# A macaron block on one core: pair 0 projected a stage earlier, ten of its maxima units in the last stages, the second phase's x split inside the last batch, and opposite bank orders for even and odd batches

## The reference, cut to what matters

```python
x = x + 0.5 * ffn(layernorm(x))        # x: 16 x 256 x 128
x = x + attn(layernorm(x))             # 16 heads of 8
x = x + 0.5 * ffn(layernorm(x))        # the same weights

def ffn(x):                            # ternary weights, one scale per output
    h = silu(tlin(x, w1)) * tlin(x, w2)        # 128 -> 512
    h = gelu(tlin(h, h1)); h = gelu(tlin(h, h2))   # 512 -> 512, exact gelu
    return tlin(h, w3)                         # 512 -> 128
def attn(x):
    q, k, v = proj(x, Wq, bq), proj(x, Wk, bk), proj(x, Wv, bv)
    return softmax(q k^T / sqrt(8)) v @ Wo.T + bo  # per head
```

## Time and profile before

| | us |
|---|---|
| median of the timed runs (3) | 666.66 (664.96 to 670.3) |
| the profiled execution's own time | 672.58 |
| its span | 670.8 |
| PE, DVE, ACT, POOL busy | 630.9, 440.4, 466.8, 92.4 |
| mean granted clock of PE | 0.949 |

### The profile page before, as it was taken

The page is one execution under the profiler, slowest core; times in us unless marked ns, Lnnn a source line. Parts: engine busy times, 40 slices in busy tenths (PEclk is TensorE's granted clock), DMA queues, the critical chain, the costliest instruction groups (busy, mean ns, idle before and its releaser), DMA issues.

```text
span 670.8 us, 12974 instructions
## 1 busy us (share of the span) xinstructions
PE 630.9 (94%) x4452; PEld 462.1 (69%) x4452; DVE 440.4 (66%) x1036; ACT 466.8 (70%) x791; POOL 92.4 (14%) x256
## 2 busy tenths in 40 slices
PE   1969999999999799999999999999999999999996
PEld 1748878788776566666666566666567878878785
DVE  4844666858545867877878887784076485656742
ACT  2646786968864357777777868774477796887964
POOL 2601010012101012222222222102001001010000
PEclk9969999999999679999999999995689999999999
DMA  9100000000051704370715343300000001001011
GB/s 296 41 2 1 1 0 0 1 0 0 1 195 56 251 2 153 101 245 13 249 62 189 118 133 127 128 1 1 1 3 1 1 0 33 0 0 31 1 31 33
DMA packets 36674, 41.97 MB, mean 63 GB/s; under 512 B 2448, under 2 KB 27280, under 8 KB 36624
## 3 DMA queue, kind: packets, MB, share of 16 engines
q1 hardware_dynamic: 36624, 41.31, 18.2%
HBM read 22.42 MB, written 18.87 MB: 62 GB/s over the span
## 4 chain that ended last, share of the span: by engine, by line
PE 82%; DVE 7%; ACT 4%; issue 3%; DMA 2%; POOL 0%; SPq 0%; ACTq 0%; POOLq 0%
PE bank L1008 45%; PE bank L1118 10%; PE bank L1092 7%; PE bank L1105 5%; PE bank L1107 4%; DVE neg_max L816 2%; PE bank L1150 2%; PE bank L1136 2%; ACT probs L630 1%; PE bank L1081 1%; PE bank L1073 1%; PE bank L1055 1%; DVE act_lo L766 1%; PE bank L1077 1%; DMA QK<-qk_scratch 1%
## 5 line engine op out<-in xcount | busy, mean ns | idle before, releaser
L1008 PE MATMUL bank<-act_hi,WH 128*128 128x512 f32 x576 | 233.3, 405 | 6.8 <-issue 5.4
L1008 PE MATMUL bank<-act_lo,WH 128*128 128x512 f32 x576 | 228.8, 397 | 0.0
L816 DVE TENSOR_REDUCE neg_max<-bank 128x2 f32<-128x512 f32 x256 | 166.9, 682 | 50.0 <-PE bank L1092 46.8
L630 ACT ACTIVATE probs<-bank 128x512 f32<-128x512 f32 x256 | 140.8, 597 | 54.6 <-PE bank L1107 52.5
L786 DVE TENSOR_TENSOR act_lo<-full,act_hi 128x512 fp32r<-128x512 f32 x128 | 88.0, 689 | 124.2 <-ACT act_hi L529 124.1
L527 ACT ACTIVATE full<-bank,SG 128x512 f32<-128x512 f32 x128 | 88.0, 687 | 69.1 <-PE bank L1008 68.7
L1008 PEld LDWEIGHTS bank<-act_hi,WH 128*128 128x128 f32 x576 | 109.1, 189 | 37.2 <-issue 6.0
L1008 PEld LDWEIGHTS bank<-act_lo,WH 128*128 128x128 f32 x576 | 109.1, 189 | 25.4 <-issue 0.5
L1105 PE MATMUL bank<-QK 32*128 32x256 f32 x512 | 113.0, 348 | 3.5 <-ACT probs L630 1.8
L1107 PE MATMUL bank<-m_parts,SEL 32*128 32x256 f32 x512 | 96.0, 293 | 0.0
L1092 PE MATMUL bank<-QK 32*128 32x256 f32 x512 | 83.1, 340 | 6.7 <-DVE neg_max L816 4.8
(11 more groups left out here) (91 smaller groups left out, 597.2 us busy)
## 6 DMA issues: line engine op xcount, KB each, us to landing
qk_scratch<-qk SPq DMA_DIRECT2D x64, 256.0 KB, 2.6
QK<-qk_scratch SPq DMA_DIRECT2D x16, 1024.0 KB, 7.2
X<-x SPq DMA_DIRECT2D x4, 512.0 KB, 6.9
raw_rest<-w_ffn SPq DMA_DIRECT2D x4, 512.0 KB, 6.1
out<-X SPq DMA_DIRECT2D x4, 512.0 KB, 3.2
raw<-w_ffn SPq DMA_DIRECT2D x3, 256.0 KB, 4.4
WA<-w_att SPq DMA_DIRECT2D x1, 256.0 KB, 5.2
xT<-sel SPq DMA_DIRECT2D x1, 256.0 KB, 5.1
```

The lines of the kernel that those rows point to most:

```text
L630: A.activation(probs[:, v % 8, :], bank[B_BANKS[v]][:, :], ACT.Exp, scale=SCALE)\
L816: D.tensor_reduce(neg_max[:, bb, qt, n0:n0 + 2], bank[banks[u]][:, :].rearrange("p (h k) -> p h k", h=2), axis=AX.X, op=ALU.max, negate=Tr ...
L1008: ins = MM(dst, a, b, start=k == 0, stop=k == len(todo) - 1)
```

## The change

- The last body of phase 0: transposes and bias product of pair 0 behind tile 0 of stage one, q behind tile 1, k behind tile 2, V behind tile 2 of stage two; the last product's high part goes ahead of the xT copy on ACT, the outputs of the body before move to its places 2 and 3. Maxima units 0 to 3 of batch 0 in stage three, 4 to 9 in stage four, 10 to 15 between the outputs.
- Pair 1's q and k go to `qk_full` and its low parts to POOL, ahead of `max_again(0, 0)`; the transposes of y come after all units.
- Bank orders: 16 units at distance three, odd batches in the opposite order; `used_last` searches through the batch before.
- V projection of the next pair (and its evacuation) from u = 7 to u = 9.
- Statistics for the second phase at u = 2 to 6 of batch 15, `normalise` at u = 10; the transposes at u = 15 of batch 15 into banks 1 and 5, ACT's split at u = 1, 2 of `attend(16)`, DVE's ahead of the addition of batch 14. POOL doubles batch 15's maxima ahead of the rsqrt. ACT's evacuation of batch 15's o is in layer 1 behind tile 0.

```diff
-A_BANKS = (0, 1, 5) * 4 + (0, 1, 5, 1)
-B_BANKS = (2, 3, 7) * 4 + (2, 3, 7, 3)
+A_BANKS = ((0, 1, 5) * 5 + (0,), (5, 1, 0) * 5 + (5,))
+B_BANKS = ((2, 3, 7) * 5 + (2,), (7, 3, 2) * 5 + (7,))
...
+        def used_last(banks, prev, u):
+            before = prev + banks[:u]
+            return next((d for d in range(1, len(before) + 1) if before[-d] == banks[u]), u + 1)
...
             pool.wait_ge(att_in, 16 * N_ATT_CONSTS)
+            low_parts(1)
             max_again(0, 0)
...
+            max_again(NBATCH - 1, 1)
             rsqrt_steps(NORMS1, K * NORMS1)
-            max_again(NBATCH - 1, 1)
...
+                        side = {0: first_x_to_sbuf, 1: lambda: high_q(0, 1), 2: first_k,
+                                3: lambda: output(before + 1, 1)}
                     hidden(g, 0, 0, side)
-                    hidden(g + HT, 0, 1, {1: lambda: high_q(0, 1), 2: lambda: high_k(0, 2)} if into_att else {})
-                    hidden(g + 2 * HT, 1, 0, {0: lambda: set_v(0, 0, 3)} if into_att else {})
+                    hidden(g + HT, 0, 1, {3: lambda: set_v(0, 0, 3)} if into_att else {})
+                    hidden(g + 2 * HT, 1, 0)
...
-                            high_q(1, 5)
-                            high_k(1, 4)
+                            full_part(1, 0, 5)
+                            high_part(1, 0)
+                            full_part(1, 1, 4)
+                            high_part(1, 1)
...
-                    layer1(t1, {3: lambda: o_to_sbuf(NBATCH - 1)})
+                    layer1(t1, {0: lambda: evacuate_o(NBATCH - 1), 3: lambda: o_to_sbuf(NBATCH - 1)})
...
-                    if u == 7 and v_pair is not None:
+                    if u == 9 and v_pair is not None:
                         set_v(*v_pair)
...
-                    if u == steps - 1 and not own:
+                    if u in (1, 2) and not own:
                         act.wait_ge(qk_written, WRITES * NPAIR)
-                        split_x(NB, 0)
-                        split_x(NB + 1, 1, 5)
+                        split_x(NB + u - 1, u - 1, (1, 5)[u - 1])
...
-                attend(2 * i + 1, 1, prev2=not first, more=more, norm=norm)
+                if more:
+                    attend(2 * i + 1, 1, prev2=not first, norm=norm)
+                else:
+                    attend(2 * i + 1, 1, more=False, steps=norm_steps(NORMS1, 0, biased=4), steps_at=2,
+                           norm=(NORMS1, 0, 8), norm_at=10)
...
+            low_x(NB, 0, 1)
+            low_x(NB + 1, 1, 5)
             add_att(NBATCH - 2, 2 * NBATCH - 4)
-            low_x(NB, 0)
-            low_x(NB + 1, 1, 5)
...
-                    hidden(g, 0, 0, h_lo, hl + HT, general, {2: tokens} if into_att else {})
+                    hidden(g, 0, 0, h_lo, hl + HT, general,
+                           {0: tokens, 1: lambda: project_q(0, 1), 2: lambda: project_k(0, 2)} if into_att else {})
...
+                    hidden(g + HT, 0, 1, h_lo, hl + 2 * HT, general, back | ({2: entry_v} if into_att else {}))
+                    hidden(g + 2 * HT, 1, 0, g_lo, g + HT + SLOTS, general,
+                           {1: lambda: entry(0), 2: lambda: entry(1, 2), 3: lambda: entry(3)} if into_att else {})
...
-                           {0: lambda: entry(0, 1), 1: lambda: entry(2), 2: lambda: entry(3, 4),
-                            3: lambda: entry(5)} if into_att else {})
+                           {0: lambda: entry(4, 5), 1: lambda: entry(6), 2: lambda: entry(7, 8),
+                            3: lambda: entry(9)} if into_att else {})
...
+                    if u == 0 and own and not prev:
+                        pe.wait_ge(q_full, 1)
+                        pe.wait_ge(k_full, 1)
...
                     if u == 1 and own and not prev:
+                        pe.wait_ge(x_added, NB + CREDIT)
                         rows_of_max()
...
-                    if u == steps - 1 and not own:
-                        pe.wait_ge(att_added, b - 1)
-                        transpose_x(XN1, 0)
+                    if u == UNITS - 1 and not more and own:
+                        transpose_x(XN1, 0, 1)
                         transpose_x(XN1 + 1, 1, 5)
-                    if u == 7 and v_pair is not None:
+                    if u == 9 and v_pair is not None:
```

More of the change, by code:

```diff
@@ L644, in o_to_sbuf, with attend @@
                 A.activation(onT[:, :], bank[6][:, 0:SEQ], ACT.Copy).then_inc(on_T_sb, 1)
-            def attend(b, prev=True, prev2=True, own=True, steps=UNITS, ahead=None, v_pair=None):
+            def attend(b, bb, prev=True, prev2=True, own=True, steps=UNITS, ahead=None, v_pair=None):
                 for u in range(steps):
@@ L651, in attend @@
                         if v < UNITS:
-                            exp_unit(b - d, v)
-                        if v == UNITS + 3:
+                            exp_unit(b - d, (bb + d) % 2, v)
+                        if v == UNITS + 3 and own:
                             evacuate_o(b - d)
@@ L682, in _ @@
             att_body(NPAIR - 1, 1, ahead=False, more=False)
-            attend(NBATCH, own=False, steps=SKEW + 4)
+            attend(NBATCH, 0, own=False, steps=SKEW + 4)
             ffn_phase(1)
@@ L816, in max_unit @@
                 D.tensor_reduce(neg_max[:, bb, qt, n0:n0 + 2],
-                                bank[banks[u]][:, :].rearrange("p (h k) -> p h k", h=2), axis=AX.X,
+                                bank[(banks or A_BANKS[bb])[u]][:, :].rearrange("p (h k) -> p h k", h=2), axis=AX.X,
                                 op=ALU.max, negate=True).then_inc(max_done, 1)
@@ L944, in _, with attend @@
             ffn_phase(0)
-            def attend(b, bb, prev=True, prev2=True, more=True, steps=(), norm=None):
+            def attend(b, bb, prev=True, prev2=True, more=True, steps=(), steps_at=7, norm=None, norm_at=3):
                 for u in range(UNITS):
@@ L956, in attend @@
                         add_att(b - 2, 2 * b - 4)
-                    if u == 3 and norm is not None:
+                    if u == norm_at and norm is not None:
                         n, tile0, width = norm
@@ L961, in attend @@
                             normalise(n, tile0 + 4, 4)
-                    if u >= 7:
-                        for step in steps[u - 7:u - 6]:
+                    if u >= steps_at:
+                        for step in steps[u - steps_at:u - steps_at + 1]:
                             step()
@@ L974, in att_body @@
                     steps, norm = norm_steps(norm_of(q), 4 * q, 4), (norm_of(q), 4 * q, 4)
-                elif not more:
-                    steps, norm = norm_steps(NORMS1, 0, biased=4), (NORMS1, 0, 8)
                 else:
@@ L1083, in project_v, with max_scores @@
                 ins.then_inc(v_mm, 1)
-            def max_scores(b, par, bb, u, banks=A_BANKS):
+            def max_scores(b, par, bb, u, banks, prev):
                 qt, jj, lane = a_unit(u)
                 rows = slice(32 * lane, 32 * lane + 32)
-                ahead = next(d for d in range(1, UNITS) if banks[u - d] == banks[u])
-                wait(pe, max_done, UNITS * b + u - ahead + 1)
+                wait(pe, max_done, UNITS * b + u - used_last(banks, prev, u) + 1)
                 for i in range(2):
@@ L1100, in scores @@
                 rows = slice(32 * lane, 32 * lane + 32)
-                last = next(d for d in range(1, UNITS) if B_BANKS[v - d] == B_BANKS[v])
-                wait(pe, exp_done, UNITS * b + v - last + 1 + CREDIT)
+                wait(pe, exp_done, UNITS * b + v - used_last(B_BANKS[bb], B_BANKS[1 - bb], v) + 1 + CREDIT)
                 for i in range(2):
-                    dst = bank[B_BANKS[v]][:, SEQ * i:SEQ * i + SEQ]
+                    dst = bank[B_BANKS[bb][v]][:, SEQ * i:SEQ * i + SEQ]
                     MM(dst, k_of(2 * par + bb)[rows, 2 * jj + i, P * kt:P * kt + P],
```

79 lines of the change are left out of this document (33 added, 46 removed).

## The result

The changed kernel takes **636.9 us** (median of four executions, 635.7 to 639.1) for 666.7 before: 29.7 us less, ratio 0.955 (0.950 to 0.960). The profiled execution has a span of 634.7 us for 670.8, so 36.1 lie between the two traces. Ratios in this document leave out executions in which the chip was in its slower state, so they can differ from the quotient of the medians.

The account below looks back on a forecast made before the run. The matrix engine, busy 94%, was taken as the bound, leaving waits, half-clock stretches and badly paired work. Gains 3.8 + 7 + 13.5 = 24.3 from 666.7 gave 642.4, so 643 us, range 632 to 659.

Parts of the forecast that it names:

- Part 3: Steady attention batches: opposite bank orders and the V projection two steps later, 0.5 us for each of 14 batches, gain 7 us.
- Part 4: End of attention: statistics leave batch 14, the clock holds in batch 15, and the tail shortens; gain 13.5 us.
- bank orders give nothing: Rival, steady batches: VectorE takes the banks' place, 1 us for 7, total 648.4; chance 0.20.
- the conversion: Profiled execution to timed runs: it stood 5.9 us above their median, so 648.3 became 642.4.
- The tail: Last units of attention after batch 15: 6.2 us at full clock, without the x transposes and the wait for the split.
- Zero, within 0.5 either way: Step into layer 1: moving o's evacuation behind its first Silu, and the Silu table load, changes nothing, within 0.5 us.
- The 2.5 for the tail's own fall: End of attention: 2.5 us taken off the gain because the tail's clock fall can come back.
- Parts 1 and 2: Entry into attention: pair 0 projected a stage earlier, ten units in stages three and four; gain 3.8 us.
- So I keep the half-clock stretch: First seam: with 2.8 of four us still idle, batch 0 keeps its 15.25 us at clock 0.50.
- The clock falls anyway: Rival, end of attention: the clock falls once the maxima end, 4.4 us for 13.5, total 651.5; chance 0.22.
- The rival at 634: The clock holds at the first seam too: 3.8 becomes 8 to 10, bank orders give 11; chance 0.10.
- The slower rival: Attention after the first seam: once down, the clock does not come back, about 705 at worst; chance 0.05.

Follow-up runs that it names:

- steady_only: The kernel before with only the opposite bank orders and the V projection at u = 9; 649.5 us, ratio 0.967.
- old_banks: The changed kernel with the bank orders of before for maxima and scores, the rest kept; 651.1 us, ratio 0.980.
- end_only: The kernel before with only the end-of-attention changes (statistics, transposes, split, evacuation of o); 664.6 us, ratio 0.999.
- fast_first: The changed kernel with PE's branch before the second phase turned round, so the path taken lies directly behind attention; 634.0 us, ratio 0.959.
- double_first: The changed kernel with GpSimd's doubling of batch 0's maxima placed between pair 1's two low parts; 637.1 us, ratio 0.963.
- entry_only: The kernel before with only the earlier projection of pair 0, ten units in stages three and four, and pair 1's low parts on GpSimd; 664.2 us.
- branch_early: The changed kernel with attention's last eight steps moved into both arms of the branch, so PE jumps earlier; 639.1 us, ratio 0.967.
- combo: fast_first plus double_first, with batch 0's scores not waiting for the second residual and m_parts computed behind the first maximum; 634.0 us, ratio 0.952.
- stats_back: The changed kernel with the statistics of the second phase's first tiles put back in batch 14; 642.7 us, ratio 0.966.

## Why the prediction was right, and where its sizes were not

The prediction, 643 us in 632 to 659 and faster by over 1%, held. Its sum of 24.3 us became 29.7, and the terms were off by more than the sum. At equal half clock the change is worth 18.8 us (656.5 less 637.7): steady part 15.8, entry 2.2, end 0.7. The other 10.4 is half-clock time, 46.5 less 17.8 us at 0.363. Together 29.2 of 29.7. That the total came so near 643 is in part luck: Part 3 gave some 9 us more than its term and the clock 10, while entry and end gave 2.9 of their 17.3 at equal half clock.

**Part 3, mis-sized: 7 became 16.** The step that failed is "I take 0.5, the middle of 0 and 1.1", with its reason, that "much of it comes back as a wait for the next maximum". A pair became 2.3 us shorter in steady_only and after alike. Taken back one at a time, the banks were worth 1.5 a pair, 0.76 a batch of the 1.1 that I had allowed at most, and V's projection, which I had counted within them, 0.65 a pair. A busy share of 83% was no bound: VectorE ran 87% in a shorter pair, and only 1.4 us of new waits in four pairs appeared, none of them for its maxima. The rival "bank orders give nothing" is refuted by old_banks.

**Part 4, right in the traces, wrong in the medians.** Between the two profiles the end gave 12.9 us for 13.5: batch 14 3.3 as predicted, batch 15 12.6 without its transposes for 12.2. But end_only gave 0.7 at equal half clock and 2 in the median. The step that failed is the conversion: the profiled execution of before stood "5.9 above the median", and I carried its 27 us of half clock at the end over to all executions as if they were the kernel's own. By the same formula it had 68 us of half clock for a median of 46.5; this difference, 22 us at 0.363, is 7.9 us. The sum carried it over, but a median execution did not have it to give.

**The tail: 8.7 us, which is the 6.2 and the 2.5 of reserve in the sum, but not for the reason given.** "Zero, within 0.5 either way" for the step into layer 1 failed: the jump left 1.56 us idle, shown by fast_first. There the same stretch, from the end of the x transposes to layer 1, takes 5.72 us at full clock, so 6.2 was about right and the jump adds 3.0. Before, the jump lay beneath work that is gone: layer 1 waited there for the split of x. The 2.5 for the tail's own fall was mis-sized the other way: the fall came, 3.4 us of it, but from the weighting before the x transposes to layer 1 after takes 10.81 us and double_first, at full clock, 10.47. That the reserve hid the missing jump is luck. The jump is also why the end is worth only 0.7 us without the clock. From the transposes of batch 15's maxima to layer 1, steady_only with the old end takes 21.02 us, all at full clock, after 21.76, fast_first 18.78: with the jump, the new end is 0.7 us longer there than the old one and gives back half of the 1.39 us that it gained at the wait; without the jump it is 2.2 shorter.

**Parts 1 and 2, right to a few tenths, and then not.** Writes at 182.58 (182.4), QK's wait 0.33 (0.1), xT's 0.73 (1.1), transposes of the maxima 221.85 (221.65), scores 223.80 (223.8): the step-by-step sum held, and GpSimd's low parts cost what its row of 1.27 us said. The reason given for keeping the stretch, 2.8 us idle in the four before the scores, was too high (1.86 in 219.80 to 223.80). "So I keep the half-clock stretch" failed: 6.8 us in the profile of after for 20.5, and 6.8 to 13.7 in the profiles of all other kernels with the new entry or the steady part, 34.1 in end_only, which has neither. That the new entry shortens it by itself is not shown: entry_only has 47.0 us of half clock in the median. Entry and end together bring 31.5 (28 to 32), all three parts 17.8 (14 to 24); the steady part alone has either 27 to 28 or 59 to 68. A half-clock time that is short in every execution was seen only with entry and end together. What in the steady part shortens the stretches stays open; no run here separates the bank orders' part in it from V's (26.0 and 25.7 with either taken back).

**The rivals.** "The clock falls anyway" in batch 15 did not happen in the profile of any kernel with the new end except where the statistics were put back; the rule in the Trainium skill on groups that cycle through PSUM banks (TensorE: Matmul & The Clock Gate, section A second HAM failure mode: psum-queue depth-cycling) spoke for that rival. The trace does not bear it out in batch 15: 13.73 us at 1.00 with the same cycling. But PE is idle for only 0.23 us there, its one wait being 0.22, so the short idle times of which the rule speaks were nearly absent. In the tail, behind a wait of 0.62 at 450.13, the clock fell, as by the rule it may. The rival at 634, with the clock at the first seam, is the one nearest the truth: the orders gave 10.7 for its 11 and V's projection 4.5 beside them, and the stretch did shorten. The slower rival, a clock that does not come back, had a real mechanism (34.1 us in end_only's first seam) but never a length that mattered: the price is 0.363 us for each us, over the 0.27 that I took from one steady group.

## What to carry to other kernels

Look for the shortest distance at which a bank is reused before trusting a neighbour's busy share as the bound: 83% busy left room for the whole gain. Where one kernel's executions differ by per cent, size what a clock fall costs from the clocks of several executions, not from the one that was traced, and compare versions at equal half-clock time. Put the side of a branch that runs directly behind it, or keep enough work queued over the jump: 1.1 us of transposes did not cover it in branch_early.

## What the runs showed of the hardware

- A branch of PE over the other copy of a long code stretch costs idle time of its own, shown as "issue". From the start of the last work ahead of it to the first behind it, eight profiles have 3.49 to 3.79 us, whether that work takes 1.07 or 1.94; the rest is idle, 1.56 to 2.72 us. With the target directly behind, it is 1.00 (fast_first, combo).
- Over 107 executions of 14 kernels, one straight line of 0.363 us for each us at the lower clock fits the times to 0.7 us. It is less than a single group loses (a weighting takes 1.94 for 1.07, so 0.45 of each us). Why is not shown; stretches that also hold other waits, as at the first seam, would lower it. One kernel's executions ranged from 30 to 86 us of it, 659 to 680 us.
- Once down, the clock can stay so for 27.3 us with PE busy all the time (before, from 452.6; stats_back, from 431.4), and for 34.1 with PE busy for 31.32 (end_only, from 220.8). Behind the same wait of 1.36 to 1.39 us it stayed down for 6.8, 17.1, 27.3 and 27.3 us in four profiles.
